# Half of a mixture-of-experts layer's second product in three split passes, and its side work moved to another time

## The chip, the core and the metric

One core of a Trainium2 chip runs the whole program. The metric is device time in microseconds (us) from launch to end, the median of the runs. Before the change it is 1193.16 us (3 runs, 1190.68 to 1193.83).

The core has five engines, each with its own instruction queue worked off in order: TensorE (PE, with its weight loads PEld), VectorE (DVE), ScalarE (ACT), GpSimd (POOL) and SyncE (SP), which only issues DMAs here. They meet through semaphores.

## The reference, cut to what matters

Attention comes first (8 batches, some 850 us) and isn't touched. Behind it stands a layer of 16 experts over T = 4096 tokens of D = 256, each expert taking its 256 best tokens:

```python
logits = xn @ router_weight.T + router_bias
probs = jax.nn.softmax(logits, axis=-1)
_, idx = jax.lax.top_k(logits.T, top_k)                     # 256 tokens for each expert
xe = xn[idx]
h = jnp.einsum('ecd,efd->ecf', xe, fc1_weight) + fc1_bias   # first product,  256 -> 1024
h = jax.nn.gelu(h, approximate=False)
y = jnp.einsum('ecf,edf->ecd', h, fc2_weight) + fc2_bias    # second product, 1024 -> 256
output = zeros.at[flat_idx].add(y * gates)                  # and divided by the sum of gates
```

All values are float32, and the result must be close to float32's.

## The kernel before, in words

**Two ways of multiplying.** TensorE takes float32 operands directly, and then the trace shows two matmul records for each product. Or an operand a is split into a rounded high part hi(a) (type F32R, by a copy on ScalarE) and a low part a - hi(a) (a subtraction), and the product is hi·hi + hi·lo + lo·hi: three passes with one record each. Before the change the first product is made in three passes, the second with float32 operands.

**One expert.** Its 256 tokens (columns) are gathered from DRAM by GpSimd's indirect DMAs (`gather`, L1257), turned by four transposes on TensorE (`turn_tokens`), and split: ScalarE makes xe_hi, VectorE xe_lo (L1666). The first product (`hidden`) has 8 steps f, each of 6 matmuls 128x128 by 128x256 into one of 4 banks. Behind each step ScalarE applies the GELU and writes h_full[f]. The second product (`expert_out`) has for each token half c = 0, 1 the 8 steps f, 128x128 of h_full by 128x256 of w2, summed in y_bank[c]. VectorE then adds the bias (`gate`, L1675), scales by the gate (`scale_out`, L1685), and GpSimd adds the rows to the output in DRAM (`scatter`, two indirect DMAs out_x, L1274).

**Side work.** The first product's weights come in as w1_raw and are split for the next expert in two halves of 128x1024: ScalarE w_hi, GpSimd w_lo (L1239, `split`). For every two experts a list of token numbers is made: on VectorE four large instructions `list_hot` (hot_hi, hot_lo, and the two hot_ids, L1629 to L1632), on TensorE 32 small matmuls `list_count`, on VectorE `list_join` (L1639, L1641), on TensorE a matmul `list_spread`, on VectorE the last three, up to token_index (L1657). The gather of these experts needs the index.

**What sets the order.** `schedule_experts` writes one plan, from which every engine takes its own pieces. For experts 1 to 15 the function `between()` adds side work at numbered points: point n stands behind the nth step, where hidden(e, 0..7) are points 1 to 8, expert_out(e, 0, ·) 9 to 16, and expert_out(e, 1, ·) 17 to 24. A point fixes only the place in each engine's own queue. Behind points 16 and 24 stands `gate`, and behind the whole expert `scale_out`.

**Buffers.** w1 (raw, hi and lo), w2, xe, h_full and y_out have two buffers, taken in turn, `gathered` has three. A load or split for expert e + 2 waits until expert e has used the buffer.

Of the kernel before, what the change touches and what calls it, by code (L numbers as in the profile page):

```python
# [236 lines left out]


def schedule_experts():
# [5 lines left out]
    def first_expert():  # L245
# [4 lines left out]
        add("list_hot", 1)  # L250
        for f in range(FT):
# [4 lines left out]
            elif f == 5:  # L256
                add("list_spread", 1)
                add("gather", 1)
                add("scale_gates")
# [28 lines left out]
    for e in range(1, E):  # L288
        lists = group_of(e + 3) if e % 2 and e + 3 < E else None
        state = {"point": 0}  # L290

        def between():
# [1574 lines left out]
```

## Time and profile before

| | |
|---|---|
| median of 3 runs | 1193.16 us |
| profiled execution: its own time | 1194.63 us |
| its span, first to last instruction | 1192.8 us |
| busy: PE, DVE, ACT, POOL | 86%, 62%, 53%, 66% of the span |
| attention | 0 to about 853 us |
| search for the experts' limits, first list | about 853 to 946 us |
| the experts | about 946 us to the end |

The profiler recorded one execution. Its span is 1.8 us shorter than the execution's own time, and that time is 1.5 us above the median. Times of rows are in us from the span's start, unless marked ns. A timeline row merges like instructions that follow one another: its length runs from the first start to the last end.

### The profile page before, as it was taken

What the parts mean: (1) busy time and instruction counts of PE and PEld (TensorE: products, weight loads), DVE (VectorE), ACT (ScalarE), POOL (GpSimd) and SP (SyncE); (2) the same over time, 40 slices, a digit from 0 to 9 for tenths busy, and PEclk for the clock granted to TensorE, in tenths of its full rate; (3) what the DMA queues carried; (4) which work ended last, traced back from release to release, by engine and by line L of the source; (5) the groups of instructions that cost most, each with busy time, mean ns of one, the idle gap of its engine ahead of it and who ended that gap; (6) DMA issues with size and microseconds to landing.
All of it is one profiled execution on the core that took longest, in us unless ns stands there. A gap on an engine that the chain in (4) does not pass through costs nothing.

```text
span 1192.8 us, 16939 instructions
## 1 busy us (share of the span) xinstructions
PE 1031.0 (86%) x5870; PEld 631.5 (53%) x5870; DVE 743.9 (62%) x1741; ACT 637.6 (53%) x1230; POOL 792.9 (66%) x891
## 2 busy tenths in 40 slices
PE   3669999999999999999999999988720498999996
PEld 2535445544644644554464464443310387888885
DVE  3676677866786876787677667783148764444411
ACT  5646656676576566667657655535224133444441
POOL 3205896797597599579759769969612166667773
PEclk9869999999999999999999999999865599999998
DMA  6020010011011011001110010010027146566652
GB/s 172 4 57 1 19 39 2 1 37 41 2 55 42 2 31 49 18 1 55 41 38 1 7 38 1 2 38 1 11 78 199 45 116 184 175 203 204 204 172 27
DMA packets 73477, 71.96 MB, mean 60 GB/s; under 512 B 38608, under 2 KB 67408, under 8 KB 69296
## 3 DMA queue, kind: packets, MB, share of 16 engines
q1 hardware_dynamic: 65392, 62.08, 16.4%
q0 software_dynamic: 6336, 8.70, 4.3%
q8 instruction: 47, 0.77, 0.3%
q10 hardware_dynamic: 1664, 0.10, 0.1%
q14 instruction: 38, 0.31, 0.1%
HBM read 56.97 MB, written 13.83 MB: 59 GB/s over the span
## 4 chain that ended last, share of the span: by engine, by line
PE 57%; POOL 21%; issue 8%; DVE 7%; ACT 4%; ACTq 1%; DMA 0%; POOLq 0%; DVEq 0%
PE bank L686 46%; POOL prob_sum L1205 8%; PE pair_bank L686 7%; POOL w_lo L1239 5%; POOL out_x L1274 4%; POOL gathered L1257 2%; ACT probs L960 2%; DVE c_in L1508 2%; PE bank L759 2%; PE bank L711 2%; DVE masked_scores L1425 1%; POOL z_lo L1184 1%; PE bank L839 1%; DVE maxima L1418 1%; ACT w_hi L960 0%
## 5 line engine op out<-in xcount | busy, mean ns | idle before, releaser
L1205 POOL TENSOR_TENSOR prob_sum<-prob_sum,probs 128x256 f32<-128x256 f32 x640 | 475.5, 774 | 81.0 <-ACT probs L960 73.9
L960 ACT ACTIVATE probs<-bank,mask_col 128x512 f32<-128x512 f32 x256 | 161.9, 685 | 110.1 <-PE bank L686 108.1
L1425 DVE CUSTOM_DVE_ANT_0 masked_scores<-pair_bank,mask_bias 128x512 bf16<-128x512 f32 x256 | 166.4, 687 | 81.5 <-PE pair_bank L686 81.4
L686 PE MATMUL bank<-probs,v_nat 128*64 128x512 f32 x768 | 205.1, 616 | 0.4 <-ACT probs L960 0.4
L1418 DVE TENSOR_REDUCE maxima<-pair_bank 128x2 f32<-128x1024 f32 x64 | 78.3, 1223 | 46.7 <-PE pair_bank L686 46.7
L960 ACT ACTIVATE probs<-bank 128x512 f32<-128x512 f32 x128 | 69.5, 595 | 66.1 <-PE bank L686 66.0
L686 PE MATMUL pair_bank<-k_hi,q_hi 64*128 64x512 f32 x384 | 92.5, 475 | 14.1 <-DVE maxima L1425 9.1
L686 PE MATMUL bank<-q_hi,k_hi 64*128 64x512 f32 x384 | 94.2, 484 | 10.7 <-ACT probs L960 8.8
L1239 POOL TENSOR_TENSOR w_lo<-w_raw,w_hi 128x1024 fp32r<-128x1024 f32 x28 | 75.1, 2683 | 38.5 <-ACT w_hi L960 38.5
L1205 POOL TENSOR_TENSOR prob_sum<-probs 128x256 f32<-128x256 f32 x64 | 44.8, 731 | 81.3 <-ACT probs L960 69.6
L1455 DVE RECIPROCAL bank<-bank 128x128 f32<-128x128 f32 x64 | 58.5, 943 | 58.4 <-PE bank L686 58.4
L686 PEld LDWEIGHTS bank<-q_hi,k_hi 64*128 64x128 f32 x384 | 37.3, 185 | 106.4 <-ACT probs L960 55.3
L686 PE MATMUL bank<-q_lo,k_hi 64*128 64x512 f32 x384 | 77.7, 394 | 0.0
L686 PE MATMUL bank<-q_hi,k_lo 64*128 64x512 f32 x384 | 77.4, 393 | 0.0
L686 PE MATMUL bank<-shift,one_rows 64*128 64x512 f32 x384 | 77.2, 391 | 0.0
L686 PEld LDWEIGHTS pair_bank<-k_hi,q_hi 64*128 64x128 f32 x384 | 37.6, 190 | 69.4 <-issue 27.4
L686 PEld LDWEIGHTS bank<-probs,v_nat 128*64 128x64 f32 x768 | 38.8, 135 | 65.0 <-issue 62.9
L960 ACT ACTIVATE h_full<-bank,b_cols 128x256 f32<-128x256 f32 x96 | 43.8, 472 | 54.2 <-PE bank L686 54.2
L1184 POOL TENSOR_TENSOR z_lo<-z_full,z_hi 128x512 fp32r<-128x512 f32 x32 | 41.1, 1284 | 46.2 <-ACT z_hi L960 46.2
L1274 POOL DMA_INDIRECT out_x<-y_out,token_index x32 | 50.9, 1591 | 21.4 <-DVE y_out L1685 11.2
L1320 DVE TENSOR_REDUCE sq_sum<-squares 128x4 f32<-128x256 f32 (+1 forms) x96 | 47.2, 496 | 25.2 <-ACT squares L960 25.2
L686 PE MATMUL pair_bank<-w,h_full 128*128 128x256 f32 x256 | 62.3, 382 | 0.0
(219 smaller groups left out, 2332.2 us busy)
## 6 DMA issues: line engine op xcount, KB each, us to landing
w_raw<-in_fc SPq DMA_DIRECT2D x16, 1024.0 KB, 4.8
w<-in_fc SPq DMA_DIRECT2D x16, 1024.0 KB, 6.9
c_in<-in_ctx SPq DMA_DIRECT2D x16, 384.0 KB, 3.4
x_in<-in_x SPq DMA_DIRECT2D x8, 512.0 KB, 5.0
out_x<-x_in SPq DMA_DIRECT2D x8, 512.0 KB, 3.5
rows_scratch<-xr_nat SPq DMA_DIRECT2D x8, 512.0 KB, 3.6
c_in<-in_ctx SPq DMA_DIRECT2D x16, 128.0 KB, 3.4
b_rows<-in_fc_bias SPq DMA_DIRECT2D x16, 128.0 KB, 7.0
```

The costliest lines, as they stand in the source:

```text
L686: return pe.matmul(out, lhsT, rhs, start=start, stop=stop, skip_group_check=True)
L711: last = pe.transpose(out[:, i * P:(i + 1) * P], src[:, i, half * P:(half + 1) * P], ident[:])
L759: last = pe.transpose(misc.bank(*use)[:, j * P:(j + 1) * P], k, ident[:])
L960: return act.activation(out, a, f, bias=bias, scale=scale)
L1184: tt(to[place][rows, half, :], z_full[rows, half, :], as32(z_hi[place][rows, half, :]), ALU.subtract).then_inc(z_lo_made.sem, 1)
L1205: last = tt(total[:, half], first[:, half], p[:, half], ALU.add)
L1239: tt(w1_lo[i][:, n, :], w1_raw[i][:, n, :], as32(w1_hi[i][:, n, :]), ALU.subtract).then_inc(w_lo_made.sem, 1)
L1274: pool.indirect_dma_start(out_rows, bass.IndirectOffsetOnAxis(ap=tokens_of(e, c), axis=0), y_out[i][:, c, :], None, compute_op=ALU.add).th ...
L1320: dve.tensor_reduce(sq_sum[:, place:place + heads], squares[square_turn[use] % 2][:, 0:heads * DH].rearrange("p (h d) -> p h d", d=DH), AX ...
L1418: last = dve.tensor_reduce(maxima[:, :, j, g], pair_bank[:], AX, ALU.max)
L1425: last = dve.tensor_tensor_reduce(masked_scores[:, hh, :], pair_bank[:, hh, :], mask_bias[:, 512 * g:512 * (g + 1)], 1.0, MASKED, ALU.add, ...
L1455: state["inverse"] = step.of(dve.reciprocal(sums, sums))
```

## The change

For experts 2 to 15 the steps f = 0 to 3 of the second product are made in three passes (`SPLIT_FROM, FS = 2, 4`). ScalarE adds a copy h_hi behind each of these four GELUs, VectorE a subtraction h_lo. For the weights ScalarE adds one copy w2_hi of 128x1024 and VectorE one subtraction w2_lo, for the next expert, at point 22. For c = 1 the steps run 4 to 7, then 0 to 3 (`OUT_ORDER`).

The side work moves. The split of w1 for e + 1 went at points 1 and 8 of expert e; now half 1 of e + 1 goes at point 9 of e, and half 0 of e + 2 at point 13. The gather of e + 2 goes from point 2 to 10. `list_hot` goes from point 1 of odd experts to points 9 and 17, in two parts; `list_count`, `list_join`, `list_spread` go from points 14, 14 and 18 of odd experts to points 2, 5 and 7 of the following even one.

```diff
+SPLIT_FROM, FS = 2, 4
+OUT_ORDER = (tuple(range(FT)), tuple(range(FS, FT)) + tuple(range(FS)))
...
         lists = group_of(e + 3) if e % 2 and e + 3 < E else None
+        counts = group_of(e + 2) if e % 2 == 0 and e + 2 < E else None
...
-            if at == 1 and lists:
-                add("list_hot", lists)
             if at == 2 and e == 1:
                 for c in range(2):
                     add("scale_out", 0, c)
-            if at == (10 if e == 1 else 4):
+            if at == 2 and counts:
+                add("list_count", counts)
+            if at == 5 and counts:
+                add("list_join", counts)
+            if at == 7 and counts:
+                add("list_spread", counts)
+            if at == (9 if e == 1 else 4):
                 for c in range(2):
                     add("scatter", e - 1, c)
-            if at == (2 if e > 1 else 9) and e + 2 < E:
+            if at == 1 and e == 1:
+                add("split", 2, 0)
+            if at == 9 and e + 1 < E:
+                add("split", e + 1, 1)
+            if at == 13 and e + 2 < E:
+                add("split", e + 2, 0)
+            if at == 10 and e + 2 < E:
                 add("gather", e + 2)
-            if at in (1, 8) and e + 1 < E:
-                add("split", e + 1, at // 8)
-            if at == 14 and lists:
-                add("list_count", lists)
-                add("list_join", lists)
-            if at == 3 * FT - 6 and lists:
-                add("list_spread", lists)
+            if at in (9, 17) and lists:
+                add("list_hot", lists, at // 17)
             if at == 3 * FT - 4 and e + 1 < E:
                 add("turn_tokens", e + 1)
+            if at == 3 * FT - 2 and e + 1 >= SPLIT_FROM and e + 1 < E:
+                add("split_out", e + 1)
...
+            if in_parts(e, f):
+                on.wait_ge(*w2_lo_made.at(e))
+                on.wait_ge(*h_lo_made.at(e, f))
+                hi, lo = h_hi[i][:, f, tokens], h_lo[i][:, f, tokens]
+                mm(to, hi, w2_hi[i][:, f, :], f == first, False)
+                mm(to, hi, w2_lo[i][:, f, :], False, False)
+                last = mm(to, lo, w2_hi[i][:, f, :], False, f == last_f)
+            else:
+                on.wait_ge(*h_made.at(e, f))
+                last = mm(to, h_full[i][:, f, tokens], w2[i][:, f, :], f == first, f == last_f)
...
+            if in_parts(e, f):
+                on.wait_ge(*h_made.at(e, f))
+                func(h_hi[e % 2][:, f, :], h_full[e % 2][:, f, :], ACT.Copy).then_inc(h_hi_made.sem, 1)
+
+        def split_out(e):
+            i = e % 2
+            on.wait_ge(w2_loaded[i], 16 * (e // 2 + 1))
+            func(w2_hi[i][:].rearrange("p f d -> p (f d)"), w2[i][:, 0:FS, :].rearrange("p f d -> p (f d)"),
+                 ACT.Copy).then_inc(w2_hi_made.sem, 1)
...
+        def split_out(e):
+            i = e % 2
+            on.wait_ge(*w2_hi_made.at(e))
+            tt(w2_lo[i][:], w2[i][:, 0:FS, :], as32(w2_hi[i][:]), ALU.subtract).then_inc(w2_lo_made.sem, 1)
+
+        def hidden(e, f):
+            i = e % 2
+            if in_parts(e, f):
+                on.wait_ge(*h_hi_made.at(e, f))
+                tt(h_lo[i][:, f, :], h_full[i][:, f, :], as32(h_hi[i][:, f, :]), ALU.subtract).then_inc(h_lo_made.sem, 1)
```

VectorE's queue before, from the end of expert 2 to the end of expert 3 (xe_lo is the tokens' low part, y_out the results):

```order
1413 L1675 TENSOR_TENSOR y_out<-pair_bank,b_rows 128x256 [waits y_filled]
1414 L1685 TENSOR_SCALAR y_out<-y_out,gate_rows 128x256 [waits gate_gathered2,y_emptied]
1415 L1685 TENSOR_SCALAR y_out<-y_out,gate_rows 128x256 [waits y_emptied]
1416 L1629 TENSOR_TENSOR hot_hi<-iota_hi,slot_hi 128x1024
1417 L1630 TENSOR_TENSOR hot_lo<-iota_lo,slot_lo 128x1024
1418 L1631 TENSOR_SCALAR hot_ids<-hot_lo,token_in_tile 128x64x16 [waits dve_step]
1419 L1632 TENSOR_TENSOR hot_ids<-hot_lo,tile_ids 128x64x16
1420 L1639 TENSOR_TENSOR list_parts<-bank,own_block 32x64 [waits listed]
1421 L1641 SCALAR_TENSOR_TENSOR list<-list_parts 32x32 [waits dve_step]
1422 L1675 TENSOR_TENSOR y_out<-bank,b_rows 128x256 [waits scattered1,expert_bias_loaded3,y_filled]
```

The same stretch of it now (w_lo<-w_1,w_hi is w2_lo):

```order
1415 L1725 TENSOR_TENSOR w_lo<-w_1,w_hi 128x1024 [waits expert_out_w_high]
1416 L1739 TENSOR_TENSOR y_out<-pair_bank,b_rows 128x256 [waits y_filled]
1417 L1749 TENSOR_SCALAR y_out<-y_out,gate_rows 128x256 [waits gate_gathered2,y_emptied]
1418 L1749 TENSOR_SCALAR y_out<-y_out,gate_rows 128x256 [waits y_emptied]
1419 L1731 TENSOR_TENSOR h_lo<-h_full,h_hi 128x256 [waits hidden_high] x4
1420 L1685 TENSOR_TENSOR hot_hi<-iota_hi,slot_hi 128x1024
1421 L1686 TENSOR_TENSOR hot_lo<-iota_lo,slot_lo 128x1024
1422 L1739 TENSOR_TENSOR y_out<-bank,b_rows 128x256 [waits expert_bias_loaded3,scattered1,y_filled,dve_step]
1423 L1678 TENSOR_SCALAR hot_ids<-hot_lo,token_in_tile 128x64x16
1424 L1679 TENSOR_TENSOR hot_ids<-hot_lo,tile_ids 128x64x16
1425 L1719 TENSOR_TENSOR xe_lo<-bank,xe_hi 128x512 [waits hidden_filled,tokens_high]
```

w2_lo stands ahead of the results' scaling, h_lo behind it, and the hot_ids have moved behind the first half's bias, ahead of the next tokens' xe_lo.

GpSimd's queue before, from expert 1's second weight half on (w_lo is a split of w1, gathered a gather, out_x a scatter):

```order
810 L1239 TENSOR_TENSOR w_lo<-w_raw,w_hi 128x1024 [waits hidden_filled,expert_w_high]
811 L1257 DMA gathered<-rows_scratch,token_index 128x272 [waits gated,index_made]
812 L1257 DMA gathered<-rows_scratch,token_index 128x272
813 L1274 DMA out_x<-y_out,token_index 4096x256 [waits scattered0]
814 L1274 DMA out_x<-y_out,token_index 4096x256
815 L1239 TENSOR_TENSOR w_lo<-w_raw,w_hi 128x1024 [waits expert_w_high]
816 L1239 TENSOR_TENSOR w_lo<-w_raw,w_hi 128x1024 [waits hidden_filled,expert_w_high]
```

Now, from the split of expert 3's first half on:

```order
810 L1290 TENSOR_TENSOR w_lo<-w_raw,w_hi 128x1024 [waits hidden_filled,expert_w_high]
811 L1325 DMA out_x<-y_out,token_index 4096x256 [waits scattered0,gated]
812 L1325 DMA out_x<-y_out,token_index 4096x256 [waits gated]
813 L1290 TENSOR_TENSOR w_lo<-w_raw,w_hi 128x1024 [waits expert_w_high]
814 L1308 DMA gathered<-rows_scratch,token_index 128x272 [waits index_made]
815 L1308 DMA gathered<-rows_scratch,token_index 128x272
816 L1290 TENSOR_TENSOR w_lo<-w_raw,w_hi 128x1024 [waits hidden_filled,expert_w_high]
```

The scatter stands ahead of the next expert's last half, and the gather between that half and the first half of the expert after it.

TensorE's queue before, around the transposes in the second product of expert 3:

```order
3018 L686 MATMUL pair_bank<-w_1,h_full 128x256 x2
3019 L918 MATMUL bank<-ident,gathered 128x128 [waits gathered0]
3020 L918 MATMUL bank<-ident,gathered 128x128 x3
3021 L686 MATMUL pair_bank<-w_1,h_full 128x256 x4
3022 L686 MATMUL bank<-xe_hi,w_hi 128x256 [waits expert_w_low,tokens_split]
```

Now, at the same place, with the first of the four steps that follow the transposes:

```order
3082 L717 MATMUL pair_bank<-w_1,h_full 128x256 x3
3083 L949 MATMUL bank<-ident,gathered 128x128 [waits gathered0]
3084 L949 MATMUL bank<-ident,gathered 128x128 x3
3085 L717 MATMUL pair_bank<-w_hi,h_hi 128x256
3086 L717 MATMUL pair_bank<-w_lo,h_hi 128x256
3087 L717 MATMUL pair_bank<-w_hi,h_lo 128x256
```

The four steps between the transposes and the next expert's first matmul are now the split ones.

## Rows read from the trace of the kernel before

**Rows 1.** Busy us by window: PE, PEld, DVE, ACT, POOL; TensorE clock, DMA share, GB/s.

```profile
997.60:1181.60 184.00, 179.62 (x1258) 162.64 (x1258) 69.06 (x109) 76.39 (x140) 123.18 (x73) 1.00 0.59 176
```

**Rows 2.** Waits of PE, 990 to 1190 us: total, times, longest.

```profile
PE bank L686 <- POOL w_lo L1239: 4.4, 7, 2.1
PE bank L686 <- DVE list L1641: 2.1, 1, 2.1
```

**Rows 3.** Chain that ended last, two places: start, length, what.

```profile
1058.25 0.96 ACT w_hi L960
...
1059.27 2.64 POOL w_lo L1239
...
1153.31 2.40 POOL w_lo L1239
```

**Rows 4.** Timeline of PE: start, length, instruction [idle before <- releaser].

```profile
997.65 0.36 PE L686 MATMUL bank<-xe_hi,w_hi 128*128 128x256 f32 x1 [2.13 <-POOL w_lo L1239]
...
1006.10 1.11 PE L686 MATMUL bank<-hot_ids,hot_hi 128*32 128x64 bf16 x32
...
1011.25 0.40 PE L686 MATMUL bank<-list,expand 32*128 32x32 f32 x2 [2.11 <-DVE list L1641]
...
1028.31 0.36 PE L686 MATMUL bank<-xe_hi,w_hi 128*128 128x256 f32 x1 [0.39 <-POOL w_lo L1239]
...
1151.42 1.89 PE L686 MATMUL pair_bank<-w,h_full 128*128 128x256 f32 x8
1153.14 0.60 PE L918 MATMUL bank<-ident,gathered 128*128 128x128 f32 x4
1153.58 1.89 PE L686 MATMUL pair_bank<-w,h_full 128*128 128x256 f32 x8
1155.85 0.36 PE L686 MATMUL bank<-xe_hi,w_hi 128*128 128x256 f32 x1 [0.37 <-POOL w_lo L1239]
1156.04 0.28 PE L686 MATMUL bank<-xe_hi,w_lo 128*128 128x256 f32 x1
1156.16 0.28 PE L686 MATMUL bank<-xe_lo,w_hi 128*128 128x256 f32 x1
```

**Rows 5.** Timeline of DVE: start, length, instruction.

```profile
1007.50 3.70 DVE L1641 SCALAR_TENSOR_TENSOR list<-list_parts 32x32 f32<-32x32 f32 x1
...
1028.30 0.60 DVE L1685 TENSOR_SCALAR y_out<-y_out,gathered 128x256 f32<-128x256 f32 x2
1028.82 1.22 DVE L1629 TENSOR_TENSOR hot_hi<-iota_hi,slot_hi 128x1024 bf16<-128x1024 f32 x1
...
1031.20 2.50 DVE L1631 TENSOR_SCALAR hot_ids<-hot_lo,token_in_tile 128x1024 bf16<-128x1024 bf16 x1
...
1154.41 0.69 DVE L1666 TENSOR_TENSOR xe_lo<-bank,xe_hi 128x512 fp32r<-128x512 f32 x1 [2.37 <-ACT xe_hi L960]
...
1181.77 0.42 DVE L1675 TENSOR_TENSOR y_out<-pair_bank,b_rows 128x256 f32<-128x256 f32 x1 [2.64 <-PE pair_bank L686]
```

**Rows 6.** Timeline of ACT: start, length, instruction.

```profile
1013.18 0.60 ACT L960 ACTIVATE xe_hi<-bank 128x512 fp32r<-128x512 f32 x1 [8.14 <-PE bank L918]
...
1029.29 0.47 ACT L960 ACTIVATE h_full<-bank,b_cols 128x256 f32<-128x256 f32 x1 [2.47 <-PE bank L686]
```

**Rows 7.** Timeline of POOL: start, length, instruction.

```profile
974.02 4.66 POOL L1239 TENSOR_TENSOR w_lo<-w_raw,w_hi 128x1024 fp32r<-128x1024 f32 x2
...
1008.23 2.91 POOL L1239 TENSOR_TENSOR w_lo<-w_raw,w_hi 128x1024 fp32r<-128x1024 f32 x1
...
1030.79 2.63 POOL L1239 TENSOR_TENSOR w_lo<-w_raw,w_hi 128x1024 fp32r<-128x1024 f32 x1 [2.63 <-ACT w_hi L960]
...
1034.90 0.97 POOL L1257 DMA_INDIRECT gathered<-rows_scratch,token_index  x1 [0.30 <-issue]
...
1081.16 1.57 POOL L1274 DMA_INDIRECT out_x<-y_out,token_index  x1 [0.30 <-issue]
```

**Rows 8.** Line 1641: min, median and maximum duration in ns.

```profile
L1641 DVE SCALAR_TENSOR_TENSOR list<-list_parts x9: 161/179/3697, 936.2 to 1123.6; 32x32 f32<-32x32 f32 x7, 16x16 f32<-16x16 f32 x2
```

More of the change, by code:

```diff
@@ L263, in first_expert @@
         for c in range(2):
-            for f in range(FT):
+            for n, f in enumerate(OUT_ORDER[c]):
                 add("expert_out", 0, c, f)
-                if c and f == 4:
+                if c and n == 4:
                     add("list_count", 2)
                     add("list_join", 2)
-                elif c and f == 6:
+                elif c and n == 6:
                     add("list_spread", 2)
@@ L283, in schedule_experts @@
     add("slots", 0)
-    for piece in ("list_hot", "list_count", "list_join", "list_spread"):
+    for part in range(2):
+        add("list_hot", 0, part)
+    for piece in ("list_count", "list_join", "list_spread"):
         add(piece, 0)
@@ L319, in schedule_experts @@
         for c in range(2):
-            for f in range(FT):
+            for f in OUT_ORDER[c]:
                 add("expert_out", e, c, f)
@@ L428, in _build @@
     w1_hi, w1_lo = ([sb(f"w1_{n}{i}", [P, 2, F], F32R) for i in range(2)] for n in ("hi", "lo"))
+    w2_hi, w2_lo = ([sb(f"w2_{n}{i}", [P, FS, D], F32R) for i in range(2)] for n in ("hi", "lo"))
+    h_hi, h_lo = ([sb(f"h_{n}{i}", [P, FS, CAP], F32R) for i in range(2)] for n in ("hi", "lo"))
     b1_cols = sb("b1_cols", [P, E, FT], F32)
@@ L625, in _build, with in_parts @@
     hidden_order = []
+    def in_parts(e, f):
+        return e >= SPLIT_FROM and f < FS
     for kind, *at in expert_plan:
@@ L628, in _build @@
             w_hi_made.will(*at)
+        elif kind == "split_out":
+            w2_hi_made.will(*at)
+            w2_lo_made.will(*at)
         elif kind == "list_hot":
-            ids_made.will(*at)
+            if at[1]:
+                ids_made.will(at[0])
         elif kind == "list_count":
@@ L646, in _build @@
             h_made.will(*at)
+            if in_parts(*at):
+                h_hi_made.will(*at)
+                h_lo_made.will(*at)
         elif kind == "gate":
@@ L1158, in hidden @@
                  bias=b1_cols[:, e, f:f + 1]).then_inc(h_made.sem, 1)
-        work = {"search": search, "split": split, "turn_tokens": turn_tokens, "hidden": hidden}
+            if in_parts(e, f):
[6 more added lines that the diff above has]
+                 ACT.Copy).then_inc(w2_hi_made.sem, 1)
+        work = {"search": search, "split": split, "turn_tokens": turn_tokens, "hidden": hidden,
+                "split_out": split_out}
         for kind, *at in expert_plan:
@@ L1617, in scale_gates, with list_hot @@
                ALU.mult).then_inc(gates_scaled.sem, 1)
-        def list_hot(g):
+        def list_hot(g, part):
             experts = experts_in(g)
@@ L1625, in list_hot @@
             steps16 = lambda t: t[:].unsqueeze(1).unsqueeze(1).broadcast_to(hot)
+            if part:
+                ts(hot_ids[:, :, 0:n, 0, :], hot_lo[:, :, 0:n, :], token_in_tile[:, 0:1], None, ALU.mult)
+                tt(hot_ids[:, :, 0:n, 1, :], hot_lo[:, :, 0:n, :], tile_ids[:].unsqueeze(2).unsqueeze(3).broadcast_to(hot),
+                   ALU.mult).then_inc(ids_made.sem, 1)
+                return
             on.wait_ge(choice_consts, 1)
```

22 lines of the change are left out of this document (11 added, 11 removed).

## The prediction

> **What bounds the kernel now.** I read the windows first. In the stretch from expert 3 to the end TensorE is busy 179.6 of 184 us at the full clock, GpSimd 123 us, VectorE and ScalarE far less [rows 1]. So matmul time is worth its own length there, and little idle time can be won. The waits by engine say what idle time there is: TensorE waits for w_lo of GpSimd, 7 times, and once 2.1 us for a list [rows 2]. The chain of waits shows why w_lo is late: ScalarE makes w_hi behind the first GELU of an expert, GpSimd starts w_lo only then, and behind it stand a gather and a scatter, before the second half can be made [rows 3]. TensorE's timeline gives the steps of one expert. H is the start of its first product, S of its second.
> - First product: matmuls follow each other after 0.12 us (1156.04 to 1156.16), so 48 x 0.119 = 5.71 us [rows 4].
> - Second product: eight records, four steps, take 1151.42 to 1153.14, so 0.43 us a step and 6.9 us for 16 [rows 4].
> - Transposes: 1153.14 to 1153.58, 0.44 us; the count of a list about 1.04, the spread 0.33 to 0.4 [rows 4].
>
> An expert without a list is thus 13.05 us of work. By the rows H(3) is 997.65, H(5) 1028.31, H(14) 1155.85, and the last bias starts at 1181.77 [rows 4, 5]. From H(5) to H(14) are four pairs with one list each and one expert without: 127.54 us, against 9 x 13.05 + 4 x 1.4 = 123.1 of work.
>
> **The change, part by part.** *Split passes.* A step becomes three passes. Passes of the same shape and kind already follow each other after 0.119 us in the first product, so 0.36 instead of 0.43: 0.075 us less, 0.6 for the eight steps of an expert. Fourteen experts: 8.4 us, all on TensorE, the engine that bounds. Were a pass as slow as a float32 record (0.216), a step would cost 0.65 and the change lose 24 us; the equal shapes exclude that.
>
> *The weight split.* Both w_hi now stand behind the last GELU. A GELU starts 0.2 us behind the end of its matmuls (the first one at 1029.29 where the first matmul stands at 1028.31 with its restart, and 0.71 are the matmuls) [rows 4, 6], so the first w_hi is done at S + 1.6. GpSimd: w_lo 2.4, gather 0.15 + 2.3, w_lo 2.4 [rows 7], i.e. S + 1.7 to 4.1, to 6.6, to 9.1. The first is needed at S + 7, the second an expert later. Both waits of rows 2 for w_lo go.
>
> *What is late next* is xe_lo. From the start of the transposes to its end it is 1153.14 to 1155.10, 1.96 us [rows 4, 5]. The matmuls behind the transposes took 1.73 us, the split ones take 1.43. A restart costs 0.2 (w_lo ended at 1155.71 [rows 3]; the regular rhythm, 0.12 back from 1156.04, begins at 1155.92). So c = 0 takes 3.16, c = 1 to the transposes 1.73, and the next H is S + 4.88 + 1.96 + 0.2 = S + 7.04, where TensorE's work would allow 6.75. An expert without a list takes 5.71 + 7.04 = 12.75 us.
>
> *VectorE's new work.* w2_lo has the shape of hot_hi, 1.22 us; h_lo I take at 0.42, as the bias of that width [rows 5], with 0.35 from one to the next; at most 0.69, xe_lo's of double width. The point is when it may run. The list instruction that takes 0.18 us took 3.70 once [rows 8], from 1007.50 on, while GpSimd's w_lo ended at 1011.14 [rows 5, 7]; the same engine's hot_ids took 2.50, to 1033.70, 0.28 behind the end of the w_lo that ran from 1030.79 [rows 5, 7]. So a VectorE instruction with two inputs in SBUF, or the fast single-input kind, waits for a running w_lo. xe_lo and the bias, which read PSUM, show nothing of this. w2_lo and h_lo read two SBUF tensors: I take it that they wait.
>
> The Trainium skill says the same in its page "SBUF — State Buffer", section "Who interferes with whom": an instruction of VectorE with two SBUF inputs contends with a GpSimd instruction that reads SBUF, and one with at most one SBUF input outside the fast modes doesn't. That rule speaks against this change, which adds five such instructions an expert; the trace agrees for the list instruction (3.70 against 0.18 us). Without the rule the sum would be rival A.
>
> Followed through an odd expert: the second w_lo of the expert before runs until H + 2.0. Then w2_lo to 3.25, bias 3.65, scaling 4.0 and 4.25 (two in 0.60 [rows 5]), h_lo 0 to 3 at 4.7, 5.05, 5.4, 5.8. ScalarE delivers h_hi in time: GELU 0.47 plus a copy that I take at 0.40 (the GELU of its width 0.47, xe_hi of double width 0.60 [rows 6]; from 0.3 to 0.6) is 0.87 a step, the fourth done at H + 4.4. TensorE wants them at 5.7, 6.1, 6.4, 6.8: hidden, with 1 us to spare. The scatter waits for the scaling: 4.3 to 7.8 (two of 1.6 with 0.3 between [rows 7]). The next w_lo starts there, at S + 2.1, not 1.7, and the w_lo after it ends at H' + 2.45. hot_ids waits for the first w_lo, to S + 4.5, and ends at S + 6.1, just as xe_lo gets its input: hidden, with nothing to spare.
>
> An even expert has the list: the join stands behind h_lo 3 (now 6.2) and is done at 6.65, TensorE is at the spread at 7 x 0.714 + 1.04 = 6.03 and waits 0.7 with the restart. So S = 5.71 + 1.04 + 0.33 + 0.7 = 7.8, and the expert takes 14.85, the pair 27.6.
>
> *The start.* At expert 2 GpSimd comes from the gathers of the first experts: w_lo 974.02 to 976.35 [rows 7], now the scatter of expert 0 (3.65) ahead of the second half, which ends at 982.4. H(2) is 982.6, later than the work allows (the list is gone there), S(2) = 982.6 + 5.71 + 1.37 + 0.6 = 990.3, and H(3) = 997.3.
>
> *Loads* (SP) of w1 now start at S + 4.5 of an expert and are needed some 12 us on; ScalarE's w2_hi waits for a load issued a whole expert before, with the next GELU queued behind it. Both cost nothing; if that cover goes, each microsecond that w2 lands late counts in full.
>
> **Sum.** Against before: H(3) -0.3; H(3) to H(5) 27.6 for 30.66, -3.1; H(5) to H(14) 4 x 27.6 + 12.75 = 123.15 for 127.54, -4.4; from there 12.75 + 12.02 + 0.2 = 25.0 for 25.9, -0.9. Together -8.7. The profiled execution took 1194.63 us (span 1192.8), so 1185.9; the median of the runs stands 1.5 lower, which gives 1184.5, said as 1185. Its own range, from the bounds of h_lo and h_hi, is 1181 to 1189.
>
> **Rivals.** *A: the subtractions don't wait for w_lo.* The rows that show the wait have other instructions (a small one and a fast kind), which speaks for it. Then w2_lo, h_lo and the join are done in time, and the six even experts lose 0.1 instead of 0.7: 3.6 less, 1181.
>
> *B: GpSimd and VectorE become the ring that bounds.* w_lo 2.4, 0.15, gather 2.3, 0.1, w_lo 2.4, w2_lo 1.25, bias 0.4, scaling 0.35, 0.3, scatter 3.5: 13.15 us, more than the 12.75 of an odd expert and less than the 14.85 of an even one, so in my count it is absorbed. For B: where both engines want the port, each is held up by the other (w_lo 2.63 where hot_lo ran, against 2.4), and hot_ids has no slack. With 0.4 more an expert a pair is 28.4 and one alone 13.3: -0.3 - 2.3 - 0.6 - 0.6 = -3.8, 1189.5.
>
> *C: slower, by ScalarE.* A copy h_hi waits for its own engine's GELU. If the two cost 1.5 us instead of 0.87, the GELUs end at S + 2.9, w_hi at S + 3.9, the two w_lo at S + 6.4 and 11.35, and then w2_lo to h_lo 3 (3.8) at S + 15.15: the next S is S + 14.1, a pair 30.3. -0.3 - 0.4 + 7.8 + 0.4 = +7.5, 1200.5. It decides from about 1.3 us a step on. Against it: 0.47 and 0.60 are the longest of the rows, and a wait in the same engine would have to cost as much again.
>
> **How the numbers follow.** Forecast 0.45, A 0.25, B 0.20, C 0.10. About 0.3%, 3.6 us, is what can be told from no change, so faster means below 1189.6: the forecast nearly whole, A, and half of B, 0.79. Same 0.11, slower 0.10. The range takes in A and B with their own spread, and leaves C out: 1178 to 1195.
>
> **What would show it.** Three passes of a step 0.36 us apart from the next; no wait for w_lo at the first matmul, but for xe_lo, about 0.3 us each; y_out rows 12.75 us apart at experts 13 to 15, and 27.6 for a pair; w2_lo starting where w_lo ends, or its length stretched to 2 us and more (A if it stays 1.2 during a w_lo); a wait of 0.7 us for the joined list in the even experts. Wrong would be a wait of TensorE for h_lo or for h_full (B, C), copies h_hi over 0.6 us, or split passes further apart than 0.12.

## The result and the profile after

| | before | after |
|---|---|---|
| median of 20 runs | 1193.49 us | 1185.43 us (1181.55 to 1190.86) |
| ratio to before | | 0.9932, interval 0.9919 to 0.9945 |
| span of the profiled execution | 1192.8 us | 1183.7 us |
| granted clock, mean over the span | 0.944 | 0.939 |
| one expert without a list | 13.05 us (13.65 at experts 13 and 14) | 12.69 us |
| a pair of experts in the steady stretch | 28.48 us | 27.13 us |

The change makes the kernel 0.68% faster, 8.1 us, where 1185 was predicted. The stretch of [rows 1], TensorE's waits in it [rows 2], and the work of one expert [rows 4 to 7] read as follows afterwards. First the busy time (PE, PEld, DVE, ACT, POOL; clock; DMA share; GB/s) of the steady stretch, and the waits of PE from 950 us on (total, times, longest):

```profile
1000.00:1172.60 172.60, 172.60 (x1360) 162.51 (x1358) 109.08 (x175) 105.33 (x203) 125.01 (x73) 1.00 0.61 185
```

```profile
PE bank L717 <- POOL w_lo L1290: 3.6, 1, 3.6
PE bank L717 <- DVE hot_ids L1679: 1.1, 1, 1.1
...
```

From 1000 us on PE is busy throughout by this count, against 179.62 of 184 before. What is left of waiting stands ahead of that. In place of the seven waits for w_lo of [rows 2] there is one long one, at expert 2. VectorE and ScalarE carry some 40 and 30 us more, and it costs nothing: neither h_lo, h_hi, w2_lo nor the joined list has a wait in the list.

The timeline of PE (start, length, instruction) at the seam from expert 3 to expert 4 shows the passes. (Of the 12 passes from 1010.50 on the last two stand here.)

```profile
1011.77 0.28 PE L717 MATMUL pair_bank<-w_lo,h_hi 128*128 128x256 f32 x1
1011.89 0.28 PE L717 MATMUL pair_bank<-w_hi,h_lo 128*128 128x256 f32 x1
1012.15 0.39 PE L717 MATMUL bank<-xe_hi,w_hi 128*128 128x256 f32 x1
1012.38 0.28 PE L717 MATMUL bank<-xe_hi,w_lo 128*128 128x256 f32 x1
...
1013.76 1.11 PE L717 MATMUL bank<-hot_ids,hot_hi 128*32 128x64 bf16 x32
1014.80 0.39 PE L717 MATMUL bank<-xe_hi,w_hi 128*128 128x256 f32 x1
...
1018.56 0.40 PE L717 MATMUL bank<-list,expand 32*128 32x32 f32 x2
```

A pass follows another after 0.12 us, so a step takes 0.36 instead of 0.43. From the last pass to the first of the next expert are 0.26 us instead of 0.12, and 0.23 from that one to the next (1012.38): together 0.25 us more than the rhythm. That is the late xe_lo, as e4 shows. The timeline of DVE through the same expert 3 (H = 999.46) and into expert 4 (H = 1012.15):

```profile
999.66 2.94 DVE L1725 TENSOR_TENSOR w_lo<-w,w_hi 128x1024 fp32r<-128x1024 f32 x1 [0.26 <-ACT w_hi L1001]
...
1003.38 1.42 DVE L1731 TENSOR_TENSOR h_lo<-h_full,h_hi 128x256 fp32r<-128x256 f32 x4
1004.72 1.21 DVE L1685 TENSOR_TENSOR hot_hi<-iota_hi,slot_hi 128x1024 bf16<-128x1024 f32 x1
1005.86 1.21 DVE L1686 TENSOR_TENSOR hot_lo<-iota_lo,slot_lo 128x1024 bf16<-128x1024 f32 x1
...
1009.01 1.06 DVE L1678 TENSOR_SCALAR hot_ids<-hot_lo,token_in_tile 128x1024 bf16<-128x1024 bf16 x1
1009.99 1.21 DVE L1679 TENSOR_TENSOR hot_ids<-hot_lo,tile_ids 128x1024 bf16<-128x1024 bf16 x1
1011.41 0.69 DVE L1719 TENSOR_TENSOR xe_lo<-bank,xe_hi 128x512 fp32r<-128x512 f32 x1 [0.21 <-ACT xe_hi L1001]
1012.35 3.40 DVE L1725 TENSOR_TENSOR w_lo<-w,w_hi 128x1024 fp32r<-128x1024 f32 x1 [0.26 <-ACT w_hi L1001]
...
1018.18 0.18 DVE L1694 SCALAR_TENSOR_TENSOR list<-list_parts 32x32 f32<-32x32 f32 x1
```

(The trace names w2_lo by its source, `w_lo<-w,w_hi`, line 1725.) And GpSimd beside it:

```profile
999.11 2.40 POOL L1290 TENSOR_TENSOR w_lo<-w_raw,w_hi 128x1024 fp32r<-128x1024 f32 x1
...
1005.60 1.79 POOL L1325 DMA_INDIRECT out_x<-y_out,token_index  x1 [0.30 <-issue]
1006.96 2.81 POOL L1290 TENSOR_TENSOR w_lo<-w_raw,w_hi 128x1024 fp32r<-128x1024 f32 x1
...
1012.26 2.40 POOL L1290 TENSOR_TENSOR w_lo<-w_raw,w_hi 128x1024 fp32r<-128x1024 f32 x1
```

w2_lo takes 2.94 and 3.40 us and ends 1.09 us behind GpSimd's w_lo both times (1002.60 and 1001.51; 1015.75 and 1014.66). At experts 5 to 14 it is the same (2.93 to 3.40 us, 1.09 or 1.10 behind). The second hot_ids ends at 1011.20, 0.2 us before xe_lo starts.

The one long wait, and what follows it, by PE's timeline at expert 2 and the windows behind it:

```profile
983.54 0.36 PE L717 MATMUL bank<-xe_hi,w_hi 128*128 128x256 f32 x1 [3.61 <-POOL w_lo L1290]
...
984.65 0.42 PE L717 MATMUL bank<-xe_hi,w_lo 128*128 128x256 f32 x1
984.87 0.41 PE L717 MATMUL bank<-xe_lo,w_hi 128*128 128x256 f32 x1
```

```profile
984.00:987.60 3.60, 3.60 (x43) 3.36 (x41) 2.66 (x6) 1.78 (x4) 3.29 (x3) 0.53 0.83 303
987.60:990.00 2.40, 2.40 (x22) 2.34 (x20) 2.37 (x2) 1.25 (x3) 2.23 (x2) 1.00 1.01 411
```

Behind 3.6 idle microseconds the granted clock falls to about half, 1.2 of 2.4 GHz, and matmuls follow each other after 0.21 us instead of 0.12, until 987.6. Such a fall isn't certain: behind 3.2 idle microseconds at the same place e6 has the clock at 1.00 (from 981.07 to 987).

### The profile page after: what moved, and what is told of

Read it like the earlier page. It is cut to its first block, busy times and chain, and to the rows that moved or that the text cites. A ratio compares the mean times of both kernels' runs of the same rounds, so it can differ in the third digit from the quotient of the medians.

```text
span 1183.7 us, 17328 instructions
## 1 busy us (share of the span) xinstructions
PE 1027.0 (87%) x5982; PEld 634.1 (54%) x5982; DVE 785.5 (66%) x1811; ACT 671.8 (57%) x1300; POOL 797.3 (67%) x891
## 4 chain that ended last, share of the span: by engine, by line
PE 72%; POOL 10%; DVE 7%; issue 5%; ACT 4%; ACTq 1%; DMA 0%; POOLq 0%; DVEq 0%
PE bank L717 55%; PE pair_bank L717 12%; POOL prob_sum L1256 8%; ACT probs L1001 2%; DVE c_in L1559 2%; PE bank L790 2%; PE bank L742 2%; DVE masked_scores L1476 1%; PE bank L870 1%; POOL z_lo L1235 1%; PE bank L949 1%; DVE maxima L1469 1%; PE bank L778 0%; ACT c_in L1001 0%; POOL gate_rows L1315 0%
## 5 line engine op out<-in xcount | busy, mean ns | idle before, releaser
L1325 POOL DMA_INDIRECT out_x<-y_out,token_index x32 | 54.7, 1709 | 39.1 <-DVE y_out L1749 34.2
L1290 POOL TENSOR_TENSOR w_lo<-w_raw,w_hi 128x1024 fp32r<-128x1024 f32 x28 | 70.0, 2500 | 7.0 <-ACT w_hi L1001 6.7
L717 PE MATMUL bank<-xe_hi,w_hi 128*128 128x256 f32 x192 | 57.6, 300 | 5.0 <-POOL w_lo L1290 3.6
```

Of the source, the lines that this page charges most:

```text
L717: return pe.matmul(out, lhsT, rhs, start=start, stop=stop, skip_group_check=True)
L1290: tt(w1_lo[i][:, n, :], w1_raw[i][:, n, :], as32(w1_hi[i][:, n, :]), ALU.subtract).then_inc(w_lo_made.sem, 1)
L1325: pool.indirect_dma_start(out_rows, bass.IndirectOffsetOnAxis(ap=tokens_of(e, c), axis=0), y_out[i][:, c, :], None, compute_op=ALU.add).th ...
```

## The experiments

All were timed in five rounds against the kernel before on the same chip. The medians of the kernel before were 1195.35 us beside the first four, 1196.25 beside the next four, and 1214.6 (1204.66 to 1228.85) beside the last three; those three are therefore compared with each other and by their traces. T(1) to the end is the stretch from the transposes at the end of expert 1 to the last bias, in the profiled execution; odd and even are one expert, from transposes to transposes, in the steady stretch. An odd expert has no list, an even one has; in the kernel before and in e2 it is the other way round, so that T(1) to the end compares these two with each other. All can be compared from T(0), the transposes at the end of expert 0: 221.40 us before, 217.46 in e1, 211.80 in the change. In e4, e8 and e9 T(1) itself lies a step earlier, and from T(0) e4 takes 210.35 us, e5 209.60, e8 209.10 and e9 209.35.

The intervals of e3, e4 and e5 overlap that of the change, so what each of these edits does is read from its trace.

| | median us | ratio, interval | T(1) to the end | odd | even |
|---|---|---|---|---|---|
| before | 1193.49 | 1 | 201.68 | 15.43 | 13.04 |
| the change | 1185.43 | 0.9932 (0.9919 to 0.9945) | 195.20 | 12.69 | 14.44 |
| e1 moves alone | 1190.87 | 0.9962 (0.9944 to 0.9980) | 200.86 | 13.04 | 14.80 |
| e2 passes alone | 1218.26 | 1.0195 (1.0168 to 1.0222) | 225.09 | 20.40 to 22.23 | 12.70 |
| e3 other order at the start | 1185.52 | 0.9918 (0.9896 to 0.9941) | 196.21 | 12.69 | 14.43 |
| e4 transposes a step earlier | 1183.85 | 0.9905 (0.9881 to 0.9928) | 194.18 | 12.46 | 14.45 |
| e5 expert 2 without passes | 1183.76 | 0.9908 (0.9879 to 0.9936) | 193.01 | 12.69 | 14.44 |
| e6 six steps in passes | 1205.26 | 1.0095 (1.0065 to 1.0124) | 211.38 | 12.41 | 17.79 (8 and 12: 18.80, 18.84) |
| e7 half 0 of w1 apart | 1199.54 | 1.0037 (1.0018 to 1.0055) | 206.95 | 12.69 | 16.20 to 17.66 |
| e8 e4 and e5 together | 1181.43 | 0.9891 (0.9861 to 0.9922) | 192.94 | 12.45 | 14.21 |
| e9 e8, whole list at point 9 | 1186.99 | 0.9819 (0.9764 to 0.9874) | 191.69 | 12.45 | 14.20 |
| e10 six steps, list at point 9 | 1206.86 | 0.9960 (0.9929 to 0.9990) | 211.05 | 12.41 | 17.77 to 20.16 |
| e11 e9 with six steps | 1199.79 | 0.9894 (0.9862 to 0.9926) | 204.90 | 12.17 | 16.84 to 18.19 |

**Which half of the change does it?** e1 keeps every move of the side work and makes no step in passes. e2 keeps the passes and puts the side work back at its old points.

```diff
e1:
-SPLIT_FROM, FS = 2, 4
+SPLIT_FROM, FS = 99, 4
e2 (list_hot, counts, join, spread, gather and split as before the change):
-            if at == 9 and e + 1 < E:
-                add("split", e + 1, 1)
-            if at == 13 and e + 2 < E:
-                add("split", e + 2, 0)
+            if at in (1, 8) and e + 1 < E:
+                add("split", e + 1, at // 8)
```

> The changed kernel without the split passes: every expert's second product with float32 operands, side work at its new points. Theory (the passes are worth their 0.075 us a step on TensorE, but a part is given back because the tokens' low part xe_lo comes 0.3 us too late behind the shorter steps, and some 0.3 us at the joined list in six experts): 8.4 us of TensorE work come back, some 3.8 and 1.8 of waits go, so 1188 us, an expert without a list 13.05 to 13.1 us. Rival (the passes bring their whole 8.4 us and more): 1194, as the kernel before. Rival (VectorE's and GpSimd's new contention costs what the passes bring): 1185 or less.

> The split passes as in the changed kernel, but all side work at its old points. Theory (the moves carry the passes: GpSimd's chain of w_hi, w_lo, gather, scatter, w_lo sets the expert at 13.65 us and is made longer by the copy h_hi ahead of w_hi; in odd experts the four list instructions of 6 us stand ahead of h_lo and TensorE waits 3 us): slower than the kernel before, about 1210 us. Rival (passes and moves bring their parts independently): 1186 to 1190.

The moves alone bring 0.38% of the 0.68%; from T(0) on they bring 3.9 us, and the passes on top of them 5.7. Each expert of e1 is 0.35 us longer than with the passes, where the prediction has 0.60 - 0.30. The 1.8 us that the expectation gave to the joined list are not there (below). The passes at the old points are slower than before by 2%, 23.4 us by T(1) to the end, in the direction expected and by more. TensorE's waits of e2 from 970 us on (total, times, longest) say by what, and DVE's rows of one place why:

```profile
PE bank L719 <- DVE h_lo L1733: 12.0, 5, 2.6
PE bank L719 <- POOL w_lo L1292: 11.4, 7, 2.7
PE bank L719 <- DVE list L1696: 6.0, 4, 1.6
```

```profile
1054.85 2.58 DVE L1733 TENSOR_TENSOR h_lo<-h_full,h_hi 128x256 fp32r<-128x256 f32 x3 [1.12 <-ACT h_hi L1003]
...
1068.71 3.42 DVE L1688 TENSOR_TENSOR hot_lo<-iota_lo,slot_lo 128x1024 bf16<-128x1024 f32 x1
```

Three h_lo take 2.58 us beside w_lo (GpSimd 1054.09 to 1056.49) and 1.1 otherwise. hot_lo takes 3.42 beside another one, with the next h_lo queued behind it. So the passes pay only with side work moved: in these rows h_lo meets w_lo and the list instructions in the time of the first product. Which of the moves it takes wasn't run one by one.

**Do the subtractions wait for w_lo?** The row of w2_lo has it stretched, but a cause needs the other case. e7 makes half 0 of w1 in the first product of the expert before its use, so that no w_lo of GpSimd runs where w2_lo starts.

```diff
-            if at == 13 and e + 2 < E:
-                add("split", e + 2, 0)
+            if at == 5 and e > 1 and e + 1 < E:
+                add("split", e + 1, 0)
```

> The changed kernel with the first weight half of expert e + 1 split at point 5 of e, not at point 13 of e - 1. Theory (VectorE's two-input subtractions wait for a running w_lo): w2_lo takes 1.1 to 1.3 us for 2.9, since no w_lo runs at the expert's start; but in odd experts the list instructions meet two w_lo, hot_ids is done 2 us later and xe_lo with it, so odd experts take 14.7 us for 12.69 and the kernel 1197. Rival (w2_lo's length is its own, of its operands): it stays at 2.9 us, and odd experts are as before.

DVE of e7 around one seam, and GpSimd's w_lo:

```profile
1058.81 1.23 DVE L1725 TENSOR_TENSOR w_lo<-w,w_hi 128x1024 fp32r<-128x1024 f32 x1 [0.26 <-ACT w_hi L1001]
...
1064.55 5.88 DVE L1686 TENSOR_TENSOR hot_lo<-iota_lo,slot_lo 128x1024 bf16<-128x1024 f32 x1
...
1072.94 1.22 DVE L1725 TENSOR_TENSOR w_lo<-w,w_hi 128x1024 fp32r<-128x1024 f32 x1
```

```profile
1064.39 4.96 POOL L1290 TENSOR_TENSOR w_lo<-w_raw,w_hi 128x1024 fp32r<-128x1024 f32 x2
```

Without a w_lo beside it w2_lo takes 1.22 or 1.23 us at all 14 experts, and the wait has moved to hot_lo, which now meets both w_lo and lasts 5.88. That makes xe_lo late (five waits, 8.8 us in all) and the kernel slower than before. Counted from H to H an odd expert takes 14.45 us (14.7 expected); from transposes to transposes that wait falls into the even one. Of the five, each behind a wait of 1.75 to 1.77 us, the two with the clock down afterwards (0.61 and 0.68) take 17.65 and 17.66 us, the three with the clock at 1.00 take 16.20 to 16.22. Rival A is out, and that the instruction ends its own length behind a w_lo beside it, and isn't long without one, is shown from both sides. The Trainium skill, page "SBUF — State Buffer", section "Who interferes with whom", has this as contention of a VectorE instruction with two SBUF inputs with a GpSimd instruction that reads SBUF. The runs agree: 1.23 against 2.94 and 3.40 us.

**The start.** In e3 GpSimd makes both halves of w1 for expert 2 before the scatter of expert 0, which aims at the wait of 3.6 us.

```diff
-            if at == (9 if e == 1 else 4):
+            if at == (10 if e == 1 else 4):
```

> The changed kernel with the scatter of expert 0 behind, not ahead of, the split of expert 2's second weight half. Theory (TensorE stood 3.6 us at expert 2 for this half, and its clock was at half for the next 3.7 us, which cost some 1.5 more): the wait goes, the clock stays up, 5 us less, 1180; some of it is given back because ScalarE's w2_hi waits for a load that lands only at 982.2 and the GELU stands behind it. Rival (that GELU is then late by the same time): 1184 to 1185.

PE's two waits in that stretch, and DVE:

```profile
980.56 0.38 PE L717 MATMUL bank<-xe_hi,w_hi 128*128 128x256 f32 x1 [1.39 <-DVE xe_lo L1719]
989.42 0.40 PE L717 MATMUL bank<-list,expand 32*128 32x32 f32 x2 [2.38 <-DVE list L1694]
```

```profile
975.71 3.06 DVE L1678 TENSOR_SCALAR hot_ids<-hot_lo,token_in_tile 128x1024 bf16<-128x1024 bf16 x1
...
984.23 3.45 DVE L1749 TENSOR_SCALAR y_out<-y_out,gate_rows 128x256 f32<-128x256 f32 x2
```

The wait for w_lo is gone and expert 2 takes 20.18 us (976.84 to 997.02) for 19.84: hot_ids stood behind the two w_lo (973.81 to 978.47), and the scaling, fast with its single input, behind the next (984.86 to 987.26). The list came late in its turn, and behind that wait of 2.38 us the clock was at 0.50 from 991 to 993 us. The rival of this run is what came out.

e5 makes expert 2 without passes, has both parts of the list at point 9 of expert 1, and scatters later in experts 1 and 2.

```diff
-SPLIT_FROM, FS = 2, 4
+SPLIT_FROM, FS = 3, 4
-            if at == (9 if e == 1 else 4):
+            if at == (10 if e < 3 else 4):
-            if at in (9, 17) and lists:
-                add("list_hot", lists, at // 17)
+            if at == 9 and lists:
+                add("list_hot", lists, 0)
+            if at == (9 if e == 1 else 17) and lists:
+                add("list_hot", lists, 1)
```

> The changed kernel with another start: the scatters of experts 0 and 1 behind the next expert's second weight half (point 10), both parts of list_hot of expert 1 at point 9, the split passes from expert 3 on. Theory (the chain that replaced the wait at expert 2 was: hot_ids behind two w_lo, w2_hi behind its load, scaling and h_lo behind the third w_lo, join behind h_lo): all of it goes, TensorE's clock stays up, from the transposes of expert 1 to those of expert 2 14.8 us for 19.84, so 5 us less, 1180. Rival (another wait takes its place again, a scatter or a load): 1184 to 1185.

Expert 2 now takes 14.89 us (981.19 to 996.08), with the clock at 1.00 from 971.7 to 1000. But expert 4 takes 17.14 for 14.44, with one wait of 2.6 us for xe_lo at its head, behind which the clock stays at 1.00 (1013.43 to 1017). Of the 5 us found, 2.7 are given back two experts later; by T(1) to the end 2.2 remain, where 5 were expected.

**The slack of xe_lo.** e4 makes the transposes one step of the second product earlier.

```diff
-            if at == 3 * FT - 4 and e + 1 < E:
+            if at == 3 * FT - 5 and e + 1 < E:
```

> The changed kernel with the transposes of the next tokens one step (0.43 us) earlier, at point 19 of 24 for 20. Theory (xe_lo is the last to come at each expert's start and TensorE loses 0.2 to 0.3 us there, 13 times): 2 to 3.5 us less, 1182 to 1183; in odd experts only in part, since xe_lo then waits for hot_ids. Rival (these gaps are not of xe_lo): 1185, no change.

An odd expert takes 12.46 us for 12.69. An even one doesn't gain: it still takes 14.45. From T(0) to the end it is 1.45 us, less than the 2 to 3.5 expected. e8 takes e4 and e5 together and puts list_spread a point later (8 for 7), and there the even one takes 14.21.

> The start of the run before together with the transposes one step earlier (point 19) and list_spread at point 8 for 7. Theory (the parts add): 5 us at the start, 0.24 at each of 12 experts, and the 0.26 us that even experts wait for the joined list when the transposes are early: 9 us less than the changed kernel, 1176.5; odd experts 12.45, even 14.2. Rival (with less work on TensorE the ring of GpSimd and VectorE, 13.0 us plus 1.1 for ScalarE's w_hi in even experts, bounds): a pair stays at 26.9, 1178.

1181.43 us, 1.1% below before. The pair in the steady stretch is 28.48 us before, 27.84 in e1, 27.13 in the change, 26.90 in e4 and 26.66 here. Most of what it missed of the expected time is expert 4: 18.53 us (1003.87 to 1022.40). It has the wait of e5 at its head (2.62 us for xe_lo, where hot_ids took 4.71 us and ended 1.08 us behind a w_lo), but here the clock is at 0.53 from 1010 to 1013.6, and it takes 1.39 us more than the 17.14 of e5.

e9 aims at that, with both parts of the list at point 9 for every expert, so that hot_ids is made before w_lo starts.

```diff
-            if at == (9 if e == 1 else 17) and lists:
+            if at == 9 and lists:
                 add("list_hot", lists, 1)
```

> The run e8_together with both parts of list_hot at point 9 in all odd experts. Theory (what was left of its gain at experts 3 to 4, 18.5 us for 14.2, was hot_ids behind a late w_lo, xe_lo behind hot_ids and TensorE's clock falling in that wait): 4.3 us less than e8_together, some 1177; from the transposes of expert 3 to those of expert 4 14.2 us. Rival (hot_ids at point 9 holds up w_lo and the later gather instead): as e8_together or slower, 1181 to 1184.

DVE and GpSimd of e9 at expert 3, and PE:

```profile
998.50 3.86 DVE L1732 TENSOR_TENSOR h_lo<-h_full,h_hi 128x256 fp32r<-128x256 f32 x3 [0.38 <-ACT h_hi L1002]
...
1003.42 1.21 DVE L1687 TENSOR_TENSOR hot_lo<-iota_lo,slot_lo 128x1024 bf16<-128x1024 f32 x1
...
1005.08 4.54 DVE L1680 TENSOR_TENSOR hot_ids<-hot_lo,tile_ids 128x1024 bf16<-128x1024 bf16 x1
```

```profile
999.00 2.40 POOL L1291 TENSOR_TENSOR w_lo<-w_raw,w_hi 128x1024 fp32r<-128x1024 f32 x1
...
1003.50 2.59 POOL L1326 DMA_INDIRECT out_x<-y_out,token_index  x1 [0.30 <-issue]
1005.54 2.98 POOL L1291 TENSOR_TENSOR w_lo<-w_raw,w_hi 128x1024 fp32r<-128x1024 f32 x1
```

```profile
1010.60 0.39 PE L718 MATMUL bank<-xe_hi,w_hi 128*128 128x256 f32 x1 [2.16 <-DVE xe_lo L1720]
```

Expert 4 takes 18.09 instead of 18.53, again with the clock at half behind its wait (0.50 from 1012 to 1015): the gain wasn't there. hot_ids stands earlier in the queue, but h_lo had waited for the w_lo before it, and so hot_ids meets the next one all the same. T(1) to the end is 1.25 us shorter than in e8, but expert 1 is 1.50 longer (17.66 for 16.16), so from T(0) e9 gains nothing; its median is not comparable with that of e8, since the chip was another one.

On that chip expert 1 takes 17.66 us in e9, 23.85 in e10 and 23.10 in e11, against 16.16 to 16.60 in all other runs with the moved side work. TensorE stands there between matmuls of the first product for up to 1.9 us, and the profile names no other engine for it. The plan of e8 and e9 is the same up to there, so it isn't the edits, and T(1) to the end leaves it out.

**Six steps instead of four.** If a pass saves 0.075 us a step, six steps should save 4 us more.

```diff
e6:
-SPLIT_FROM, FS = 2, 4
+SPLIT_FROM, FS = 2, 6
```

> The changed kernel with six of eight steps in split passes. Theory (the ring of GpSimd and VectorE: w_lo 2.40, 0.16, gather 2.33, w_lo 2.40, w2_lo to the scatter 1.97, scatter 3.75 = 13.0 us, and w2_lo half as long again makes it 13.55): a pair of experts stays at 27.1 us, no gain, 1185. Rival (the passes add up: 4 more steps' worth, 0.3 us an expert): pair 26.5, 1181.

1205.26 us, 20 more than with four, and outside what either theory gave. PE's waits of e6 from 970 us on, then one seam: DVE, GpSimd, PE.

```profile
PE bank L717 <- DVE xe_lo L1719: 13.3, 5, 2.7
PE bank L717 <- DVE list L1694: 4.9, 6, 1.1
PE bank L717 <- POOL w_lo L1290: 3.2, 1, 3.2
PE bank L717 <- DVE h_lo L1731: 0.4, 1, 0.4
```

```profile
1063.54 1.21 DVE L1685 TENSOR_TENSOR hot_hi<-iota_hi,slot_hi 128x1024 bf16<-128x1024 f32 x1
1064.68 1.22 DVE L1686 TENSOR_TENSOR hot_lo<-iota_lo,slot_lo 128x1024 bf16<-128x1024 f32 x1
...
1066.27 3.79 DVE L1678 TENSOR_SCALAR hot_ids<-hot_lo,token_in_tile 128x1024 bf16<-128x1024 bf16 x1
```

```profile
1063.75 3.60 POOL L1325 DMA_INDIRECT out_x<-y_out,token_index  x1 [0.30 <-issue]
1066.80 2.97 POOL L1290 TENSOR_TENSOR w_lo<-w_raw,w_hi 128x1024 fp32r<-128x1024 f32 x1
```

```profile
1071.85 0.58 PE L717 MATMUL bank<-xe_hi,w_hi 128*128 128x256 f32 x1 [2.64 <-DVE xe_lo L1719]
```

w2_lo is half as long again (128x1536) and two more h_lo follow it, so hot_hi starts at H + 6.8 us instead of H + 5.3. In the change the second scatter also runs beside hot_hi and hot_lo, but hot_hi is 0.88 us under way when it starts, and it takes 1.79 us. Here hot_hi is 0.21 us under way, and it takes 3.60. w_lo starts later for it, hot_ids ends only at 1070.06, 0.29 us behind w_lo, and xe_lo, queued behind, is 2.6 us late. This wait, 2.64 to 2.67 us, stands at the head of five even experts, 4 to 12. The clock behind it isn't always the same (windows as above, at expert 4 and at expert 8):

```profile
1011.48:1014.50 3.02, 3.02 (x47) 2.84 (x48) 3.02 (x1) 1.67 (x4) 2.77 (x2) 1.00 1.01 420
...
1072.00:1075.00 3.00, 3.00 (x20) 2.78 (x20) 3.00 (x1) 1.08 (x3) 2.63 (x2) 0.52 1.02 428
```

At experts 4, 6 and 10 it stays at 1.00 and the expert takes 17.79 us, at 8 and 12 it is at half and the expert takes 18.80 and 18.84. A pair takes 30.2 us (12.41 and 17.79) or 31.2 where 27.13 was. So the waits make most of the loss: at 1.00 an even expert is 3.35 us longer than in the change, from 2.65 us for xe_lo and 0.88 for the joined list, less the 0.3 that the passes save. The clock adds 1.0 at two experts.

e10 gives six steps the list at point 9, e11 is e9 with six steps.

```diff
e10, against e6:
-            if at in (9, 17) and lists:
-                add("list_hot", lists, at // 17)
+            if at == 9 and lists:
+                add("list_hot", lists, 0)
+                add("list_hot", lists, 1)
```

> Six steps in split passes as in e6_six_steps, with both parts of list_hot at point 9. Theory (the 20 us that e6_six_steps lost come from hot_ids, held by a w_lo that had slipped, and from the clock that fell in each wait of 2.6 us for xe_lo): nearly all of it comes back, a pair of experts at 27.0 to 27.5 us, 1184 to 1187. Rival (VectorE's longer work for six steps itself is too much): a pair stays near 30 us, 1200 or more.

> Six steps with everything of e9_all_at_9. Theory (the ring of GpSimd and VectorE, 13.5 us and more, now bounds): a pair at 27.0 to 27.5 us for 26.66, so 2 to 4 us slower than e9_all_at_9, 1179 to 1181. Rival (the passes add up, 0.3 us an expert): 4 us faster than e9_all_at_9, 1173.

Neither helps; e10 is what its rival said, and e11 is slower than both its theories. TensorE waits for xe_lo 13.2 us in e10 and 12.1 in e11, five times each, and from T(1) to the end e11 takes 13.2 us more than e9 (204.90 and 191.69). The scatter takes 3.60 us five times in e10 and four times in e11. So moving the list instructions to point 9 isn't enough: with six steps VectorE is still inside them when w_lo starts. Which further edit would give six steps room wasn't tried.

## Why the prediction came out right

The profiled execution is 9.1 us shorter in span, where the sum gives 8.7. By the prediction's own terms:

| | predicted | measured |
|---|---|---|
| H(3) | -0.3 | +1.8 (999.46 for 997.65) |
| H(3) to H(5) | -3.1 | -3.5 (27.13 for 30.66) |
| H(5) to H(14) | -4.4 | -6.3 (121.22 for 127.54) |
| H(14) to the last bias | -0.9 | -0.9 (25.00 for 25.92) |
| sum | -8.7 | -9.0 |

The size is right in part because two errors cancel: the start cost 2.1 us more than the sum had, and the stretch from H(3) to H(14) gained 2.3 more.

- **Split passes**: 0.36 for 0.43 us a step, as predicted; e1 against the change shows them in an odd expert as 0.35 us, the part that xe_lo doesn't take back (0.30 predicted).
- **The moves**: both waits for w_lo go in the steady stretch. e2 shows that without them the passes lose.
- **xe_lo late next**: right, as 0.25 us more than the rhythm over two matmuls; the odd expert takes 12.69 for the predicted 12.75. e4 shows the other side: earlier transposes give 0.23 back.
- **VectorE waits for a running w_lo**: right, by e7. w2_lo ends at H + 3.14 (3.25 predicted), hot_ids at 1011.20, S + 6.0 (6.1 predicted), "with nothing to spare". e6 shows what this phrase meant: 20 us. One of the rows that the prediction rests on is weaker than it was read: the list instruction of [rows 5] starts at 1007.50, 0.73 us before the w_lo of [rows 7] (1008.23), while a scatter was under way (1007.19 to 1008.76), so it did not only wait for a w_lo that was running.
- **h_lo 0.42 and h_hi 0.40**: measured 0.42 and 0.42, and 0.82 us from one GELU to the next with its copy (0.87 predicted). Rival C is out, with the widths it needed (1.3 and more).
- **Loads at no cost**: no wait of TensorE hangs on them. ScalarE's w2_hi of expert 2 waited 3.40 us for its load, beside the wait for w_lo, which hid it.
- **Even expert, wait of 0.7 us for the joined list**: wrong. The list is joined at 1018.36, H + 6.2 instead of 6.65, because the last h_lo ends at H + 5.9, not 6.2, and the join takes 0.33 us, not 0.45, and TensorE comes to the spread only at H + 6.4 and finds it there. In its place 0.38 us stood that the sum had left out: what count and spread cost beyond 1.04 and 0.33, by the changes from one form of matmul to another (0.21 and 0.22 us at 1013.76 and 1014.80 in place of 0.12). e1 has the same 1.75 us between an even and an odd expert without any h_lo, so the join costs nothing there. The even expert takes 14.44 for 14.85.
- **The start**: H(2) is 983.54 for 982.6, but GpSimd came 0.95 us later from before (974.97 for 974.02), which explains that part. The failed step is what follows: 14.7 us from H(2) to H(3) predicted, 15.92 measured. The sum had the wait for w_lo at its own length. It also cost half of the clock for 3.5 us behind it: seven matmuls at 0.21 us for 0.12 and the count (1.81 for 1.04 us), about 1.5 us. e6, where the clock stays up at this place, has 15.33.

Rival B, that the ring of GpSimd and VectorE bounds, is not what happens with four steps: TensorE is busy without a gap. It is nearest to what e6 and e7 show, where TensorE waits at each even expert for a VectorE that GpSimd has held up, and its price is too low for them: 0.4 us an expert against 3.05 us a pair of e6 with the clock at 1.00 throughout. The price lies in xe_lo queued behind a whole w_lo; the clock comes on top only at some experts.

Open remains why the clock falls behind some waits of 1.75 to 2.7 us and not behind others of the same length, which of the moves the passes need, and what stops TensorE at expert 1 on the chip of e9 to e11.

## What to carry to other kernels

Where one engine bounds, shorter matmuls are worth their length only as long as the engines that prepare operands stay inside their slack; count that slack at the last place before it ends, since two more steps (e6: two h_lo, two h_hi and half as much again of w2) turned an expected gain of up to 4 us into a loss of 20. Two engines whose instructions hold each other up must be planned as one: put them at different times, and expect a removed wait to reappear in the next instruction of that kind (e3, e5, e7). A change that is two edits is to be run as two: here the one that saves the arithmetic is slower alone.

## What the runs showed of the hardware

- A wait of TensorE can cost more than its length, and its length alone doesn't tell. The granted clock was 0.53 for 3.6 us behind 3.6 us of idle time in the change, and 1.00 behind 3.2 us at the same place in e6. Behind the wait of 2.6 to 2.7 us for xe_lo it fell at two of five experts in e6 and at four of five in e10, fell in e8 and stayed in e5; behind 1.75 us it fell at two of five in e7. Where it fell, an expert was 1.0 (e6) to 1.45 us (e7) longer than one with the same wait and the clock at 1.00. Behind the gaps of 0.26 us it stayed at 1.00.
- GpSimd's generation of a scatter isn't free of VectorE either. It takes 1.55 to 1.64 us with nothing beside it and 1.79 to 3.60 us beside hot_hi and hot_lo, by how the starts fall: 1.79 with hot_hi 0.88 us under way (the change), 2.62 with 0.10 (e1, five times), 3.60 with 0.21 (e6, e10 and e11, 14 times), 2.59 with hot_lo 0.08 under way (e9), and 1.58 where hot_hi starts 0.38 us behind it (e7). The 3.60 and the 2.59 end 1.45 or 1.46 us behind the end of hot_lo, the 2.62 end 1.51 behind that of hot_hi, as if the scatter had begun there. That it waits for such instructions fits these rows; no run took them away alone.
- VectorE's fast single-input instructions wait like the two-input ones: the scaling took 3.45 us for two instead of 0.60 in e3 while w_lo ran, and hot_ids 3.79 instead of 0.48 in e6.
- VectorE is also held by a w_lo that starts after its own instruction, by the profile's times: w2_lo of e6 starts 0.55 us before it (1071.72 and 1072.26), takes 4.55 us instead of 1.79 and ends 1.63 us behind it; hot_ids of e8 starts 0.67 us before it and takes 4.71 us instead of 1.22. GpSimd was in a gather or scatter at that time, and its times are rough, so what held VectorE in those 0.55 to 0.67 us is not shown.
